# Two groups of transposes and copies placed behind the first layer's router products

## The chip, the cores and the metric

The kernel runs on one core of one Trainium2 chip. A core has five engines that this text names: TensorE (PE; its weight loads are listed apart as PEld), VectorE (DVE), ScalarE (ACT), GpSimd (POOL) and SyncE (SP), whose queue issues most DMAs. Each engine works through its own list of instructions in order and waits for others by semaphores. The metric is the device time of one launch in microseconds (us), less is better; a median of several runs is given.

## The reference, cut to what matters

The program computes two layers of a graph network on 3125 nodes with 256 features each. A layer adds a graph convolution and an attention part to the stream `x`, then a mixture of experts. What is computed around the change is the end of the first layer's graph and attention part and the start of its experts:

```python
xn = _layernorm(x, axis=-1)
x = x + _L0_gnn_ref(xn, ...) + _L0_mix_ref(xn[None], ...)[0]
x = x + _L0_ffn_ref(_layernorm(x, axis=-1)[None], ...)[0]

def _L0_ffn_ref(x, Wr, br, W1, b1, W2, b2, gamma, beta):
    logits = jnp.mean(x, axis=1) @ Wr + br             # mean over all 3125 rows
    routing_weights = jax.nn.softmax(logits, axis=-1)
    scale = jnp.where(expected_loads > capacity, capacity / expected_loads, 1.0)
    routing_weights = jax.nn.softmax(routing_weights * scale, axis=-1)
    top_w, top_i = jax.lax.top_k(rw_tok, 2)
    top_w = jax.nn.softmax(top_w, axis=-1)
    h = jax.nn.gelu(xf @ W1[e] + b1[e], approximate=False)   # for the chosen experts
    y = h @ W2[e] + b2[e]
    out = _layer_norm(weighted sum of y + x, gamma, beta)
```

The router sees the mean of all normalised rows, so all rows choose the same two of the eight experts, and nothing of an expert's product can start before the mean over all rows is known.

## The kernel before, in words

The 3125 rows are 25 tiles of 128 rows (`T` = 25), in five groups of five (`GROUP`, `GROUPS`). `X` holds the stream, `N` the normalised rows with nodes on the partitions, `NT` the same rows transposed, with features on the partitions (`KC` = 2 blocks of 128 features). `ps` are eight banks of PSUM: three (`TA`, handed out in turn by `A.next()`) take the transposes and the experts' first products, two (`TV`) take products that VectorE adds to the stream, one (`PACC`) takes sums that stay.

The stage around the change closes the graph convolution's second hop, group by group, on four engines at once:

- VectorE closes the hop of a group, adds TensorE's products for the group before it to `X` (L1723), takes the rows' statistics (L1445 to L1450), and writes the normalised rows of the group before that into `N` (L1456), each tile telling `xn_ready`.
- ScalarE applies the relu (L1280), takes the square root for the statistics (L1221), and copies transposed rows from PSUM into `NT` (`transposed_copies`, L1231), five tiles a group. Each copy frees its bank (`pa_free`) and then tells `nt_ready`.
- TensorE runs a loop over s = 0 to 6 (`for s in range(GROUPS + 2)`). For s below 5 it multiplies the hop's rows of group s by the layer's weights (`hops_out`, L947). For s of 2 and more it first transposes the normalised rows of group s - 2 (`normalised_transposed`, L818: two transposes for a tile, behind a wait for `xn_ready` and for a free bank), then adds the same rows to the column sums in `PACC` (L959: two products of 128x128 by 128x1 for a tile, listed as four matmuls, since an f32 product is two passes). In the last two turns, s = 5 and 6, there is no hop product left, only transposes and column sums of groups 3 and 4.

Then follows the router, a chain that no engine can shorten by overlap. TensorE tells `route_mm`; VectorE scales the column sums into `ybar` (L1757); TensorE multiplies them by the router's weights (L967); VectorE adds the bias, asks ScalarE for an exponential (`softmax`, L1733 to L1738, ScalarE's side is `exp`, L1226), limits the weights to the capacity, does a second softmax with a second exponential, finds the best two (L1772, L1773), asks for a third exponential (of one number for each partition, L1774) and computes the row numbers of the two experts' weights (L1780 to L1782). GpSimd then issues 16 gathers of weights (L770); the first three (two of the first layer's weights, one of biases) let TensorE start the first expert's first product (L981), the others the second expert and the second layer. TensorE waits for all `nt_ready` of the pass ahead of L981, since its moving operand is `NT`. The third exponential's answer is needed only for the scaling of the second layer's weights (L1787 to L1792), which stands behind the last of these gathers.

ScalarE's list in this stretch is: relu, root and copies for s = 0 to 6, then `exp`, `exp`, `exp`, then the gelu of L981's products (L1310).

Of the kernel before, what the change touches and what calls it, by code (L numbers as in the profile page):

```python
# [36 lines left out]
T = -(-NODES // P)  # L37
# [20 lines left out]
GROUPS = T // GROUP  # L58
# [53 lines left out]
def build(nc, a, out):  # L112
    with ExitStack() as ctx:
# [3 lines left out]
        def sem(name):  # L117
            return ctx.enter_context(nc.semaphore(name))
# [57 lines left out]
        xn_ready, nt_ready = sem("xn_ready"), sem("nt_ready")  # L176
# [196 lines left out]
        def group(g):  # L373
            return range(g * GROUP, (g + 1) * GROUP)
# [427 lines left out]
        def _(pe):  # L802
# [10 lines left out]
            def normalised_transposed(first, g, src=N):  # L813
                for t in group(g):
                    pe.wait_ge(xn_ready, first * T + t + 1)
                    o = A.next()
                    for c in range(KC):
                        mm = nc.tensor.transpose(o[:, c * P:(c + 1) * P], src[:, t, c * P:(c + 1) * P], ident[:, :])  # L818
                    mm.then_inc(pa_full, 1)
# [121 lines left out]
            def hops_out(t):  # L941

                if t % GROUP == 0:
                    pe.wait_ge(relu_ready, t // GROUP + 1)
                o = V.next()
                for c in range(KC):
                    mm = nc.tensor.matmul(o[:, 0:D], AT[:, c, t * P:(t + 1) * P], wgT[:, c, :], start=(c == 0), stop=(c == KC - 1))  # L947
                mm.then_inc(pv_full, 1)

            for s in range(GROUPS + 2):  # L950
                if s < GROUPS:
                    for t in group(s):
                        hops_out(t)
                if s >= 2:
                    normalised_transposed(1, s - 2)

                    for t in group(s - 2):
                        for c in range(KC):
                            mm = nc.tensor.matmul(PACC[:, c:c + 1], N[:, t, c * P:(c + 1) * P], valid[:, t:t + 1],  # L959
                                                  start=(t == 0 and c == 0), stop=(t == T - 1), skip_group_check=True)  # L960
# [5 lines left out]
            for c in range(KC):  # L966
                mm = nc.tensor.matmul(PACC[:, 8:8 + E0], ybar[:, c, :], wr[:, c, :], start=(c == 0), stop=(c == KC - 1))  # L967
            mm.then_inc(route_mm, 1)
            pe.wait_ge(nt_ready, 2 * T)
            first_done = [0] * GROUPS  # L970
            for g in range(GROUPS + 1):
# [240 lines left out]
        def _(act):  # L1212
# [4 lines left out]
            def root(v):  # L1217

                roots[0] += 1
                act.wait_ge(asked, roots[0])  # L1220
                nc.scalar.activation(v, v, ACT.Sqrt).then_inc(answered, 1)  # L1221

            def exp(v):
                roots[0] += 1
                act.wait_ge(asked, roots[0])
                nc.scalar.activation(v, v, ACT.Exp).then_inc(answered, 1)  # L1226

            def transposed_copies(tiles):
                for t in tiles:
                    o = A.next()  # L1230
                    nc.scalar.copy(NT[:, :, t * P:(t + 1) * P], o[:, 0:D].rearrange("p (c n) -> p c n", n=P)).then_inc(pa_free, 1)  # L1231
                    act.wait_ge(pa_free, A.n)
                    act.sem_inc(nt_ready, 1)
# [42 lines left out]
            for s in range(GROUPS + 2):  # L1276
                if s < GROUPS:
                    act.wait_ge(slice_ready, GROUPS + s + 1)
                    part = AT[:, 0:KC, s * GN:(s + 1) * GN]
                    nc.scalar.activation(part, part, ACT.Relu).then_inc(relu_ready, 1)  # L1280
                if 1 <= s <= GROUPS:
                    root(rstd[:, (s - 1) * GROUP:s * GROUP])
                if s >= 2:
                    transposed_copies(group(s - 2))


            exp(sc[:, 0:8])
            exp(sc[:, 0:8])
            exp(sc[:, 40:41])
            def squares(src, tiles, dump):  # L1290

                for t in tiles:
                    st.settle()
                    st.add(nc.scalar.activation(dump, src[:, t, :], ACT.Square, accum_out=rn[:, t:t + 1]))
# [853 lines left out]
```

## Time and profile before

| what | us |
|---|---|
| median of 3 runs (lowest, highest) | 2977.78 (2976.58, 2977.94) |
| the profiled execution's own time | 2973.64 |
| its span, from the first to the last instruction | 2971.8 |
| PE busy | 2477.6 (83% of the span) |
| DVE busy | 1303.0 (44%) |
| POOL busy | 884.5 (30%) |
| ACT busy | 454.1 (15%) |

The mean granted TensorE clock was 0.922 of full speed. In the rows below each line gives a start, a duration, the engine, the line of the kernel, the operation, what it writes and reads, the shape and how many instructions were merged (x20); in brackets stands how long the engine was idle before it and what released it. The clock column (PEclk) is 1.00 at TensorE's upper level of 2.4 GHz and 0.50 at its lower level of 1.2 GHz.

### The profile page before, as it was taken

Reading aid. Unit: us, or ns where it says so; the run is one execution under the profiler, and the core shown is the slowest. Engines: PE = TensorE matmul, PEld = TensorE weight load, DVE = VectorE, ACT = ScalarE, POOL = GpSimd, SP = SyncE. Lnnn points to the kernel's source line nnn. Section 1 sums busy time; section 2 is a strip of 40 time slices with the busy share of each in tenths; the row PEclk is TensorE's granted clock in tenths of the full one; section 3 lists DMA queues with packets and bytes.
Section 4 is the critical chain, followed back from the end, with each engine's and each line's share of the span. In section 5 each row is a group of like instructions: output and inputs, shape, how many; then the busy total and the mean of one; then the engine's idle time right before and its main releaser. Section 6 shows DMA issues by size and latency. Waiting matters only on the chain.

```text
span 2971.8 us, 33705 instructions
## 1 busy us (share of the span) xinstructions
PE 2477.6 (83%) x12264; PEld 1722.4 (58%) x12264; DVE 1303.0 (44%) x3539; ACT 454.1 (15%) x963; POOL 884.5 (30%) x917
## 2 busy tenths in 40 slices
PE   4567777776766766589969998999999998999999
PEld 3455655655555555567845565565555556566665
DVE  8887867766765757433482214131000003131221
ACT  0211110111000000022331103330000010413222
POOL 0177777774777777320030000120000000000000
PEclk9989998997888879769989999999999999989999
DMA  3134344343344344210022220022111000000001
GB/s 105 57 100 135 103 138 139 105 140 109 104 140 140 104 140 125 72 49 1 18 76 71 79 77 29 32 99 65 50 51 56 29 1 21 1 11 11 11 11 44
DMA packets 77650, 211.87 MB, mean 71 GB/s; under 512 B 16445, under 2 KB 33845, under 8 KB 76073
## 3 DMA queue, kind: packets, MB, share of 16 engines
q0 software_dynamic: 40800, 111.47, 12.7%
q1 hardware_dynamic: 36681, 98.17, 10.0%
q8 instruction: 103, 1.69, 0.2%
q14 instruction: 66, 0.54, 0.1%
HBM read 169.10 MB, written 40.47 MB: 71 GB/s over the span
## 4 chain that ended last, share of the span: by engine, by line
PE 64%; DVE 16%; DMA 7%; issue 5%; POOL 3%; ACT 2%; DVEq 1%; SPq 0%; ACTq 0%; POOLq 0%
PE ps L1114 16%; PE ps L1150 13%; DMA rows<-table,src_i 7%; PE ps L555 7%; PE ps L1086 7%; PE ps L1208 5%; POOL rows L494 3%; PE ps L981 3%; PE ps L992 3%; DVE onehot L674 2%; DVE NN L1671 2%; DVE NN L1659 2%; PE ps L880 1%; DVE NN L1660 1%; DVE NN L1682 1%
## 5 line engine op out<-in xcount | busy, mean ns | idle before, releaser
L494 POOL DMA_INDIRECT rows<-table,src_i x832 | 812.5, 977 | 389.2 <-issue 296.6
L555 PE MATMUL ps<-onehot,rows 128*128 128x128 f32 x3328 | 551.1, 308 | 212.4 <-DMA rows<-table,src_i 178.0
L555 PEld LDWEIGHTS ps<-onehot,rows 128*128 128x128 f32 x3328 | 524.3, 220 | 319.5 <-issue 206.2
L1114 PE MATMUL ps<-AS,WA 128*128 128x400 f32 (+1 forms) x768 | 259.7, 501 | 11.5 <-ACT NN L1352 5.1
L880 PE MATMUL ps<-NN 128*128 128x500 bf16 x416 | 170.7, 410 | 114.9 <-DVE NN L1660 99.4
L674 DVE TENSOR_SCALAR onehot<-iota_w,rel,wgt 128x128 f32<-128x128 f32 x848 | 231.1, 358 | 2.8 <-DVE iota_w L714 1.6
L1114 PEld LDWEIGHTS ps<-AS,WA 128*128 128x128 f32 x768 | 148.6, 194 | 121.4 <-issue 5.8
L1114 PE MATMUL ps<-NN,WA 128*128 128x400 f32 (+1 forms) x640 | 213.3, 495 | 1.0 <-ACT rows L1365 0.7
L2086 DVE SCALAR_TENSOR_TENSOR X<-ps,WA,X 128x256 f32<-128x256 f32 x150 | 72.5, 484 | 272.0 <-PE ps L1208 272.0
L1352 ACT ACTIVATE AS<-ps,small 128x400 f32<-128x400 f32 (+1 forms) x224 | 131.2, 586 | 334.4 <-PE ps L1114 334.4
L1114 PEld LDWEIGHTS ps<-NN,WA 128*128 128x128 f32 x640 | 122.1, 191 | 89.0 <-issue 1.3
L2030 DVE SCALAR_TENSOR_TENSOR AS<-ps,small,AS 128x408 f32 x32 | 20.3, 643 | 347.2 <-PE ps L1150 346.4
L692 DVE TENSOR_TENSOR AS<-AS,ps 128x256 f32 x104 | 43.8, 421 | 279.7 <-PE ps L555 279.7
L1671 DVE TENSOR_TENSOR NN<-NN,ps 128x500 f32 x208 | 140.0, 673 | 53.4 <-issue 22.6
L1659 DVE TENSOR_SCALAR NN<-WB,AS 128x500 bf16<-128x500 f16 x416 | 150.3, 361 | 0.3
L1150 PE MATMUL ps<-WA,NN 128*128 128x408 bf16 x768 | 137.1, 336 | 0.0
L1150 PE MATMUL ps<-onehot,NN 128*128 128x408 bf16 x768 | 136.1, 336 | 0.0
L1208 PE MATMUL ps<-WA,AS 128*128 128x256 f32 x600 | 135.5, 388 | 0.0
L880 PEld LDWEIGHTS ps<-NN 128*128 128x128 bf16 x416 | 43.9, 105 | 138.7 <-DVE NN L1671 97.8
L1208 PEld LDWEIGHTS ps<-WA,AS 128*128 128x128 f32 x600 | 104.0, 191 | 31.5 <-issue 13.2
L1660 DVE TENSOR_SCALAR NN<-WB,AS 128x128 bf16<-128x128 f16 x416 | 113.7, 273 | 0.0
L1723 DVE TENSOR_TENSOR X<-X,ps 128x256 f32<-128x256 f32 x100 | 41.2, 417 | 162.4 <-PE ps L1170 112.2
(353 smaller groups left out, 3055.2 us busy)
## 6 DMA issues: line engine op xcount, KB each, us to landing
adjacency<-NN SPq DMA_DIRECT2D x8, 2550.0 KB, 9.1
onehot<-adjacency SPq DMA_DIRECT2D x40, 510.0 KB, 3.5
WA<-adjacency SPq DMA_DIRECT2D x40, 510.0 KB, 3.5
rows<-table,src_i POOLq DMA_INDIRECT x832, 2.8
table<-NN SPq DMA_DIRECT2D x10, 640.0 KB, 3.3
table<-WA SPq DMA_DIRECT2D x25, 256.0 KB, 2.0
WA<-in_experts SPq DMA_DIRECT2D x6, 768.0 KB, 4.1
X<-in_x SPq DMA_DIRECT2D x1, 3072.0 KB
```

The lines of the kernel that those rows point to most:

```text
L494: nc.gpsimd.indirect_dma_start(slot_of(h, j, k), None, table[h - 1][:, :], bass.IndirectOffsetOnAxis(index, 0)).then_inc(gathered[h - 1][( ...
L555: mm = nc.tensor.matmul(EDGE[j % 2][:, c * P:(c + 1) * P], row[:, c * P:(c + 1) * P], onehot[:, j % 2 * U + k, :], start=(k == 0 and c == ...
L674: nc.vector.tensor_scalar(onehot[:, buffer * U + k, :], iota_w[:, :], rel[:, bass.ds(c, 1)], wgt[:, bass.ds(c, 1)], ALU.is_equal, ALU.mult ...
L880: nc.tensor.matmul(build_bank(s)[:, 0:CELLS], sources_in[:, n % CELL_RING, :], cells[:, n % CELL_RING, :], start=(j == 0), stop=(j == 1)). ...
L1086: mm = nc.tensor.matmul(EDGE[c][:, 0:SLABW], rows16, pieces[i % 4][:, n, :], start=(t == 0 and part == 0), stop=(t == T - 1 and part == 2))
L1114: mm = nc.tensor.matmul(o[:, 0:n.stop - n.start], weights[:, k, c * P:(c + 1) * P], src[:, k, n], start=(k == 0), stop=(k == chunks - 1))
L1150: mm = nc.tensor.matmul(banks[c][:, 0:SLABW], hidden16(t)[:, part, f], pieces[i % 4][:, n, :], start=(t == 0 and part == 0), stop=(t == T ...
L1208: mm = nc.tensor.matmul(o[:, 0:D], h2[:, k, t * P:(t + 1) * P], w[:, 2, k, :], start=(k == 0), stop=(k == KC - 1))
L1352: nc.scalar.activation(dst[:, c, n], o[:, 0:n.stop - n.start], ACT.Relu, bias=bias[:, c:c + 1]).then_inc(pa_free, 1)
L1659: nc.vector.tensor_scalar(cells[:, n % CELL_RING, :], iota500, cell_of[:, n:n + 1], None, ALU.is_equal).then_inc(cells_ready, 1)
L1660: nc.vector.tensor_scalar(sources_in[:, n % CELL_RING, :], iota500[:, 0:P], source_in[:, n:n + 1], None, ALU.is_equal).then_inc(cells_read ...
L1671: nc.vector.tensor_tensor(part, part, build_bank(s)[:, 0:CELLS].rearrange("p (t n) -> p t n", n=SUBW), ALU.add).then_inc(slab_added, 1)
```

## The change

In TensorE's loop the transposes of groups 3 and 4 are left out (`2 <= s < GROUPS` covers groups 0 to 2 only) and stand behind the router's products instead. The column sums stay, and since no transposes with their wait stand ahead of them now, each tile's column sums get a wait of their own for `xn_ready` (in all five groups). ScalarE's ten copies of groups 3 and 4 move too: two tiles behind the first exponential, the other eight behind the second one, ahead of the third.

```diff
@@ TensorE @@
                     for t in group(s):
                         hops_out(t)
+                if 2 <= s < GROUPS:
+                    normalised_transposed(1, s - 2)
                 if s >= 2:
-                    normalised_transposed(1, s - 2)
-
                     for t in group(s - 2):
+                        pe.wait_ge(xn_ready, T + t + 1)
                         for c in range(KC):
                             mm = nc.tensor.matmul(PACC[:, c:c + 1], N[:, t, c * P:(c + 1) * P], valid[:, t:t + 1],
                                                   start=(t == 0 and c == 0), stop=(t == T - 1), skip_group_check=True)
...
             mm.then_inc(route_mm, 1)
+            for g in range(GROUPS - 2, GROUPS):
+                normalised_transposed(1, g)
             pe.wait_ge(nt_ready, 2 * T)
@@ ScalarE @@
                 if 1 <= s <= GROUPS:
                     root(rstd[:, (s - 1) * GROUP:s * GROUP])
-                if s >= 2:
+                if 2 <= s < GROUPS:
                     transposed_copies(group(s - 2))


             exp(sc[:, 0:8])
+            transposed_copies(group(GROUPS - 2)[0:2])
             exp(sc[:, 0:8])
+            transposed_copies(group(GROUPS - 2)[2:])
+            transposed_copies(group(GROUPS - 1))
             exp(sc[:, 40:41])
```

## Rows read from the trace of the kernel before

**Rows 1.** The page's chain of waits by engine, over the whole span.
```profile
PE 64%; DVE 16%; DMA 7%; issue 5%; POOL 3%; ACT 2%; DVEq 1%; SPq 0%; ACTq 0%; POOLq 0%
```

**Rows 2.** The chain of waits in order of time, 1292.71 to 1358.63 (start, us, what).
```profile
1292.71 2.13 PE ps L959 x20
...
1296.81 4.06 PE ps L959 x20
1300.87 2.24 PE ps L818 x10
1303.10 4.07 PE ps L959 x20
...
1308.82 12.43 issue
1321.25 37.38 PE ps L981 x128
```

**Rows 3.** Timeline of GpSimd: the first and the third gather of the experts' weights.
```profile
1316.15 0.94 POOL L770 DMA_INDIRECT WA<-in_w_rows,small  x1 [88.59 <-DVEq L1784]
...
1318.65 0.94 POOL L770 DMA_INDIRECT small<-in_b_rows,small  x1 [0.30 <-issue]
```

**Rows 4.** Timeline of VectorE, 1295 to 1340.
```profile
1295.91 1.71 DVE L1456 TENSOR_SCALAR NN<-X,small 128x256 f32<-128x256 f32 x5
...
1315.37 0.15 DVE L1787 TENSOR_SCALAR small<-small 128x1 f32<-128x1 f32 x1
...
1339.04 0.75 DVE L1792 TENSOR_SCALAR WA<-WA,small 128x1024 f32<-128x1024 f32 x1 [23.12 <-DMA rows<-in_b_rows,small]
```

**Rows 5.** Timeline of ScalarE, 1301 to 1332.
```profile
1301.43 2.31 ACT L1231 COPY NN<-ps 128x256 f32<-128x256 f32 x5 [3.97 <-PE ps L818]
1303.84 1.28 ACT L1226 ACT_TABLE_LOAD   x1
1309.46 0.21 ACT L1226 ACTIVATE small<-small 128x8 f32<-128x8 f32 x1 [4.33 <-DVE small L1734]
1311.53 0.21 ACT L1226 ACTIVATE small<-small 128x8 f32<-128x8 f32 x1 [1.87 <-DVE small L1734]
1313.04 0.20 ACT L1226 ACTIVATE small<-small 128x1 f32<-128x1 f32 x1 [1.30 <-DVE small L1774]
...
1331.75 0.53 ACT L1310 ACTIVATE AS<-ps,small 128x320 f32<-128x320 f32 x1 [0.55 <-PE ps L981]
```

**Rows 6.** Busy time and granted clock by stretches; the first line names the columns.
```profile
core 0: us, PE busy (x) PEld busy (x) DVE busy (x) ACT busy (x) POOL busy (x), PEclk, DMA share, GB/s
...
1257.00:1261.50 4.50, 0.26 (x2) 0.00 (x0) 4.39 (x16) 0.21 (x1) 0.00 (x0) 1.00 0.00 0
1262.00:1263.40 1.40, 0.00 (x0) 0.00 (x0) 1.40 (x2) 0.00 (x0) 0.00 (x0) 0.50 0.00 0
1238.10:1241.20 3.10, 3.10 (x8) 2.47 (x9) 1.91 (x2) 1.27 (x1) 0.00 (x0) 0.50 0.00 0
...
1295.50:1296.00 0.50, 0.46 (x4) 0.20 (x2) 0.46 (x3) 0.39 (x2) 0.00 (x0) 0.96 0.88 353
...
1296.50:1301.00 4.50, 4.50 (x24) 4.50 (x23) 1.12 (x4) 0.75 (x2) 0.00 (x0) 0.50 0.20 79
...
1321.20:1326.20 5.00, 4.95 (x10) 3.22 (x11) 0.00 (x0) 2.11 (x3) 3.78 (x5) 0.50 0.47 132
```

**Rows 7.** Timeline of TensorE's weight loads, 1300 to 1303.
```profile
1300.52 2.18 PEld L818 LDWEIGHTS ps<-ident,NN 128*128 128x128 f32 x10
```

**Rows 8.** Timeline of ScalarE, 1597 to 1605: a copy that stands between two exponentials.
```profile
1604.25 0.27 ACT L1337 COPY VB<-ps 128x128 f32<-128x128 f32 x1
1604.67 0.31 ACT L1226 ACTIVATE WA<-WA 128x128 f32<-128x128 f32 x1 [0.16 <-DVE WA L1883]
```

**Rows 9.** Busy time of the engines over the rest of the span (columns as in Rows 6).
```profile
1358.47:2971.80 1613.33, 1550.95 (x7042) 974.10 (x7040) 387.02 (x903) 324.10 (x686) 55.08 (x55) 0.97 0.12 39
```

## The prediction

> **What bounds the kernel now.** I read the chain of waits by engine first: TensorE holds 64% of it, VectorE 16% [rows 1]. Shares of the whole span don't price this change, because it touches one stretch of about 30 us; so I next read the chain in order of time there [rows 2]. The reader is to see one unbroken string: column sums of group 2 to 1294.84, then transposes of group 3 (to 1296.81, so 1.97 us), column sums of group 3 (4.06), transposes of group 4 (2.24), column sums of group 4 (4.07, ending at 1307.17), then VectorE's `ybar`, the router's four matmuls (ending at 1308.82), and 12.43 us in which TensorE stands still until L981. The view gives that gap to "issue", since DMA completions of this kind aren't linked to it. Its content is in the other engines' timelines. VectorE and ScalarE do two softmaxes and the indices; GpSimd's first gather waits for VectorE (L1784) until 1316.15, the third is issued by 1319.59 [rows 3], and 1.66 us behind that L981 starts. So L981 is released by the gathers, and the gathers by the column sums. What makes the column sums end earlier makes everything behind them start earlier.
>
> VectorE is no limit to the column sums: its last normalised row of group 4 is written by 1297.62 [rows 4], while TensorE works on those sums until 1307.17. In this stretch the transposes of groups 3 and 4 thus lie on the path that sets the end, though nobody needs them before L981.
>
> **The change, part by part.**
>
> *Transposes out of the path.* 1.97 us (group 3) and 2.24 us (group 4) leave the string [rows 2]: 4.21 us. That would be all, if the clock stood still. The same 20 matmuls of L959 took 2.13 us for group 2 and 4.06 us for group 3 [rows 2]; in between the granted clock fell from the upper level (2.4 GHz) to the lower (1.2 GHz), where it is from 1296.5 on [rows 6]. The half microsecond to 1296.0 still has 0.96, so the fall is at 1296.0. From 1294.84 to 1296.0 TensorE did transposes, which were held up by banks and by VectorE and gained little from the clock. After the change it does column sums there: 1.16 us at 2.13/20 = 0.107 us each is 11 of the 40 matmuls. The 29 left take 0.203 us each, 5.9 us, and the sums end at 1296.0 + 5.9 = 1301.9 instead of 1307.17. Gain: 5.2 us. Rows must be there: group 3's are written before 1295.91, group 4's by 1297.62 [rows 4], and TensorE reaches group 4's first tile about 1297.8; no wait binds.
> Bounds by the place of the fall. If the clock is already low at 1294.84, the two transposed groups are worth 2 x 2.24 = 4.5 us. If it falls near 1298, both kernels do most of group 3's sums at the upper level and the gain is 6.0. If it stayed high in both, the new sums would be held by VectorE and end near 1297.62 + 4 x 0.107 + some tenths, hence about 1299.1 with TensorE's own 4.3 us of work, against 1303.0 for the string of before: 3.9.
>
> *Waits added.* 25 waits for `xn_ready`, one a tile; what queues behind each is that tile's weight loads and sums. In groups 0 to 2 the transposes ahead of them have already waited for the same count. The trace has no row of L959 behind a wait, but one of L818, whose every tile has two: its weight loads for group 4 began at 1300.52, while the sums ahead of them ran until 1300.87 [rows 2, 7], so a wait that is already met doesn't stop the loading ahead. I take 0. Upper bound, if each wait lays one load bare at the lower level: 2.18/10 = 0.22 us [rows 7], for ten tiles on the path 2.2 us. A gain from a wait is excluded, it only delays.
>
> *Transposes and copies put back in the gap.* Behind the router's products TensorE runs 20 transposes: at the lower level 0.45 us a tile (2.24/5), 4.5 us of the 12.43 us gap. Three tiles go through at once, then banks pace them by ScalarE's copies, 2.31/5 = 0.46 us each [rows 5]. With R for the end of the router's products (before: 1308.82): the first exponential was at R + 0.64 to R + 0.85, and by then tile one is transposed (R + 0.45). Two copies end at R + 1.8. The second exponential was asked and began at R + 2.71: ScalarE is free 0.9 us ahead of it, so the path has nothing to pay. It ends at R + 2.92; eight copies end at R + 6.7. L981 is released at R + 12.4, so the copies are 5.7 us ahead of its wait for `nt_ready`. What pays is the third exponential: from R + 4.2 to about R + 6.8. VectorE reached the line that needs it at 1315.37 = R + 6.55 [rows 4], so it waits some 0.3 us; behind that it had 23.12 us of idle time until the second layer's weights land [rows 4], and the row numbers for the gathers stand ahead of this wait. Cost on the path 0. Were the cover gone, that delay would be the price: 0.3 us. Below nothing isn't possible, as no one waits less for it. No DMA is issued or moved by the edit, and SP's and GpSimd's lists are untouched.
>
> *Table load.* ScalarE loads its table ahead of the first exponential, at 1303.84, behind group 4's copies [rows 5]. Now it follows the last root, near 1294.3, and is even less on the path: 0.
> A reader might fear that copies between exponentials make ScalarE load a table twice more, 1.28 us each [rows 5]. At 1604.25 a copy stands right ahead of an exponential, with 0.16 us between them and no load [rows 8]; I take 0, with 2.6 us (two loads) as the other end.
>
> *What happens behind.* L981 starts 5.2 us earlier, at 1316.0. It starts at the lower level, which lasted over 5.0 us [rows 6], and its 32 banks took 37.38 us [rows 2] where banks at the upper level come every 0.53 + 0.55 = 1.08 us [rows 5], 34.5 in all: the cold start costs 2.9 us. Elsewhere a busy TensorE was granted the upper level again just after 3.1 us at the lower [rows 6], so the same start can cost about 1.6. The shift can thus bring up to 1.3 us more; I take 0, since before was near the long end in one execution and the timed runs average over it. Behind L981 TensorE is busy for 1551 of 1613 us [rows 9], and every gap there hangs on work that starts with L981; I see no transfer or engine that keeps its old time, and take the shift as whole.
>
> Sum: 4.21 (transposes) + 1.0 (sums done at the upper level in their place) + 0 + 0 + 0 = 5.2 us. The profiled execution's own time is 2973.64 us, so 2968.4 for one like it. The median of the runs is 2977.78, 4.1 us above it, so the timed forecast is 2977.8 - 5.2 = 2972.6 us. Faster or slower by over 0.2% means 5.96 us (2971.8, 2983.7), about what a measurement of this kernel can tell from no change; my number lies just inside it.
>
> **The rivals.**
>
> *The filled gap keeps the clock up.* TensorE's transposes now fill about 5.7 us of the gap. If the clock rose in them and held until L981, its cold start would vanish: 2.9 us more, 8.1 in all, 2969.7 us. Against it: at 1257 to 1261.5 the clock stayed high over some 4 us of idle TensorE and was low by 1262 [rows 6], and 6.7 us of idle are left between the last transpose and L981.
> The Trainium skill, "TensorE: Matmul & The Clock Gate", section "HAM oscillation — how this bites in real kernels", says that idle gaps send the array back to its lower clock and the next burst starts cold; by that rule a shorter gap is the only way to keep it, and the trace agrees as far as the fall at 1262 goes.
>
> *The shift is lost on the way.* Behind L981 lie 1613 us with gaps of TensorE at many places (62 us in all [rows 9]), after which the clock falls and rises at places that move with the shift. Each such start differs by up to 1.3 us, as worked out above. Three or four of them the wrong way take 4 us: 2976 to 2978 us. For it: the profiled execution and the median differ by 4.1 us with the same program. Against it: the three runs agree within 1.4.
>
> *ScalarE is late for the second exponential.* If the two copies wait for TensorE's transposes (say each tile takes 0.9 instead of 0.45 us, with semaphores), they end at R + 2.8 rather than R + 1.8; the path pays 0.1 to 1 us, with a doubled table load up to 2.6. Gain 2.6 to 4.6: 2973 to 2975 us. Against it: 0.9 us of slack, and copies had such a pace at 1301.43.
>
> *Slower: the waits break TensorE's weight loading.* Place: L959. If a wait, even a met one, stops the loading ahead and the matmul ahead must drain too, a tile pays a load and a matmul: 0.22 + 0.20 us, 25 tiles 10.5 us, against 5.2 gained: 2983 us. It decides from 0.21 us a tile on, if all 25 lie on the path; in groups 0 to 2 VectorE's sums to `X` hide part. Against it: the row of L818's loads above.
>
> **How the numbers follow.** Forecast 0.64, own range 2971.0 to 2974.5 (gain 3.9 to 6.0 by the place of the fall, up to 1.3 by L981's start, 0.5 for the runs); 0.22 of it lies below 2971.8. Clock kept up: 0.10. Lost on the way: 0.14. ScalarE late: 0.07. Slower than before: 0.05, of which half goes past 0.2%; the other half stays within. Faster by over 0.2%: 0.22 + 0.10 = 0.32. Slower: 0.03. Within: 0.65. The range reaches from 2969.0, to hold the clock rival, to 2977.0, to hold most of the lost shift and ScalarE late.
>
> **What would show it.** In the profile after: no L818 between 1294 and the router's products; L959 in one string of 60 matmuls ending near 1302, its last 29 or so at 0.2 us; `ybar` at 1302, the router's matmuls ending near 1303.6; two copies between the first two exponentials, with no table load beside them; the last copy by 1310.4; L981 at 1316, still cold; VectorE's L1787 a few tenths late. It is wrong if L959 takes over 0.25 us a matmul at the lower level (the waits), if the gap ahead of L981 is longer than 12.4 us (ScalarE or the copies), or if L981 starts near 1316 and the end doesn't come 5 us earlier (lost on the way).

## The result, and the profile after

The changed kernel takes 2971.74 us (median of 16 runs, 2968.98 to 2974.85), the kernel before on the same chip 2976.53 (16 runs, 2972.51 to 2978.27). The medians are 4.8 us apart. The ratio on record is not that of the two medians: it is 0.9986, 95% interval 0.9979 to 0.9992, hence 4.2 us less, between 2.4 and 6.3. The forecast was 2972.6 and a shift of 5.2. The profiled execution took 2970.61 us, its span is 2968.7, against 2973.64 and 2971.8.

Code lines below the edit have new numbers: the column sums are L960 (before: L959), the router's products L968 (L967), L981 and L992 are now L984 and L995, and the copies' and exponentials' lines L1234 and L1229 (L1231, L1226).

The chain of waits of the changed kernel in order of time, the answer to [rows 2]:
```profile
1293.09 9.48 PE ps L960 x60
1302.60 0.50 DVE rows L1763 x2
1303.20 1.04 PE ps L968 x4
...
1314.08 2.67 DMA small<-in_b_rows,small
1316.74 0.09 issue
1316.83 36.40 PE ps L984 x128
```
The string of five pieces has become one of 60 matmuls. This time the view also names what the gap ahead of the expert's products was: it runs through the gathers, and the landing of the biases' rows ends it.

TensorE's timeline of the changed kernel:
```profile
1291.26 1.83 PE L818 MATMUL ps<-ident,NN 128*128 128x128 f32 x10
1292.93 9.63 PE L960 MATMUL ps<-small,NN 128*128 128x1 f32 x60
1303.20 1.02 PE L968 MATMUL ps<-small,rows 128*128 128x8 f32 x4 [0.64 <-DVEq L1765]
1304.08 2.54 PE L818 MATMUL ps<-ident,NN 128*128 128x128 f32 x10
1307.56 2.60 PE L818 MATMUL ps<-ident,NN 128*128 128x128 f32 x10 [0.94 <-ACT NN L1234]
1316.83 36.40 PE L984 MATMUL ps<-NN,WA 128*128 128x320 f32 x128 [6.68 <-DMA small<-in_b_rows,small]
```
From the start of group 2's transposes to the router's first product it is 1303.20 - 1291.26 = 11.94 us; before it was 16.92 (1290.88 to 1307.80). I call this stretch the string from here on. The moved transposes take two bursts with a wait for ScalarE between them, and 6.7 us of idle time stay behind them.

ScalarE's timeline, the answer to [rows 5]:
```profile
1294.62 1.28 ACT L1229 ACT_TABLE_LOAD   x1
1304.86 0.21 ACT L1229 ACTIVATE small<-small 128x8 f32<-128x8 f32 x1 [8.95 <-DVE small L1740]
1304.97 0.84 ACT L1234 COPY NN<-ps 128x256 f32<-128x256 f32 x2
1306.94 0.21 ACT L1229 ACTIVATE small<-small 128x8 f32<-128x8 f32 x1 [1.13 <-DVE small L1740]
1307.06 3.75 ACT L1234 COPY NN<-ps 128x256 f32<-128x256 f32 x8
1310.92 0.20 ACT L1229 ACTIVATE small<-small 128x1 f32<-128x1 f32 x1
```
ScalarE was idle for 1.13 us between the second copy and the second exponential, which follows the first by 2.08 us as before (2.07 [rows 5]); there is no further table load. The eight copies end 6.0 us ahead of L984. VectorE waits for the third exponential, the cost that was to be hidden, and is (timeline of VectorE):
```profile
1311.16 0.15 DVE L1793 TENSOR_SCALAR small<-small 128x1 f32<-128x1 f32 x1 [0.51 <-ACT small L1229]
1334.32 0.75 DVE L1798 TENSOR_SCALAR WA<-WA,small 128x1024 f32<-128x1024 f32 x1 [22.56 <-DMA rows<-in_b_rows,small]
```
The clock, from the view of stretches (columns as in [rows 6]): it is at 1.00 in the sums' first 3 us, at 0.50 by 1296.8, and still at 0.50 when L984 starts.
```profile
1293.10:1296.10 3.00, 3.00 (x29) 3.00 (x29) 2.89 (x15) 2.44 (x5) 0.00 (x0) 1.00 0.68 204
1296.80:1302.50 5.70, 5.70 (x28) 5.67 (x27) 1.20 (x4) 0.00 (x0) 0.00 (x0) 0.50 0.17 64
...
1316.80:1320.20 3.40, 3.37 (x7) 2.23 (x8) 0.00 (x0) 0.81 (x1) 2.60 (x3) 0.50 0.53 155
```

The two profiled executions, piece by piece: the stretch began 0.38 us later (its start lies anywhere from 1290.48 to 1293.74 us in the traces of the experiments below, so this is no effect of the change that could be told from chance), the string is 4.98 us shorter, from the router's first product to the expert's first 0.18 longer (13.63 against 13.45), the expert's first 32 banks 0.98 shorter (36.24 against 37.22, less time at the lower clock), and all that follows 2.30 longer (1615.6 us from the first second-layer product to the end, against 1613.3). Sum: -3.1 us, the difference of the spans.

### The profile page after: what moved, and what is told of

Read it like the earlier page. It is cut to its first block, busy times and chain, and to the rows that moved or that the text cites. A ratio compares the mean times of both kernels' runs of the same rounds, so it can differ in the third digit from the quotient of the medians.

```text
span 2968.7 us, 33705 instructions
## 1 busy us (share of the span) xinstructions
PE 2483.6 (84%) x12264; PEld 1722.8 (58%) x12264; DVE 1302.5 (44%) x3539; ACT 453.9 (15%) x963; POOL 884.5 (30%) x917
## 4 chain that ended last, share of the span: by engine, by line
PE 64%; DVE 17%; DMA 7%; issue 5%; POOL 3%; ACT 2%; DVEq 1%; SPq 0%; ACTq 0%; POOLq 0%
PE ps L1117 16%; PE ps L1153 13%; DMA rows<-table,src_i 7%; PE ps L555 7%; PE ps L1089 7%; PE ps L1211 5%; POOL rows L494 3%; PE ps L984 3%; PE ps L995 3%; DVE NN L1677 2%; DVE onehot L674 2%; DVE NN L1665 2%; PE ps L880 1%; DVE NN L1666 1%; DVE NN L1688 1%
## 5 line engine op out<-in xcount | busy, mean ns | idle before, releaser
L1117 PE MATMUL ps<-AS,WA 128*128 128x400 f32 (+1 forms) x768 | 259.9, 501 | 11.4 <-ACT NN L1358 4.9
```

What stands on the lines that cost most here:

```text
L1117: mm = nc.tensor.matmul(o[:, 0:n.stop - n.start], weights[:, k, c * P:(c + 1) * P], src[:, k, n], start=(k == 0), stop=(k == chunks - 1))
```

## The experiments

Each kernel ran in five rounds beside the kernel before on one chip, in four sessions; the median of the kernel before went from 2974.90 to 2978.95 between them, so a median is compared only with one that ran beside it. e0 is the changed kernel again; e1 and e9 are edits of the kernel before, all others of the changed one. The stretches of the table are read from TensorE's timeline of each profile; "string" and "to expert" as above, "banks" is from the first product of the expert's first layer to the first of its second, "rest" from there to the end of the span. The interval is that of the ratio to before.

| kernel | string | to expert | banks | rest | median us / before | interval |
|---|---|---|---|---|---|---|
| before | 16.92 | 13.45 | 37.22 | 1613.3 | | |
| changed | 11.94 | 13.63 | 36.24 | 1615.6 | 2971.74 / 2976.53 | 0.9979 to 0.9992 |
| e0_after (changed again) | 12.20 | 13.58 | 36.00 | 1615.4 | 2972.00 / 2976.94 | 0.9977 to 0.9995 |
| e1_waits_only | 16.92 | 13.55 | 37.06 | 1613.1 | 2974.40 / 2974.90 | 0.9990 to 1.0008 |
| e2_group4_only | 14.90 | 13.55 | 36.51 | 1612.6 | 2971.70 / 2974.90 | 0.9978 to 0.9996 |
| e3_copies_first | 12.01 | 16.42 | 36.48 | 1612.5 | 2972.56 / 2974.90 | 0.9982 to 1.0000 |
| e4_copies_last | 11.94 | 13.41 | 36.35 | 1612.3 | 2969.86 / 2974.90 | 0.9972 to 0.9990 |
| e5_group2_too | 11.63 | 13.41 | 36.53 | 1612.6 | 2971.55 / 2976.94 | 0.9970 to 0.9988 |
| e7_gap_filled | 12.76 | 13.63 | 34.60 | 1615.5 | 2971.07 / 2976.94 | 0.9968 to 0.9988 |
| e9_before_wide | 12.50 | 13.25 | 35.95 | 1615.4 | 2972.18 / 2978.95 | 0.9968 to 0.9986 |
| e6_wide_sums | 9.17 | 13.19 | 37.50 | 1613.5 | 2966.73 / 2976.94 | 0.9947 to 0.9974 |
| e10_wide_again | 9.17 | 13.21 | 37.38 | 1613.4 | 2968.85 / 2978.95 | 0.9958 to 0.9979 |
| e8_wide_filled | 9.17 | 13.19 | 34.60 | 1613.4 | 2965.86 / 2978.95 | 0.9946 to 0.9973 |

(For e5 the string is counted from the start of group 2's column sums, which follow the last hop product there; in the others group 2's transposes do.)

**Do the added waits cost?** The kernel before with the waits alone:
```diff
                     for t in group(s - 2):
+                        pe.wait_ge(xn_ready, T + t + 1)
                         for c in range(KC):
```


> The kernel before with only the 25 added waits of TensorE ahead of the column sums. Theory (the gain is the 4.2 us of transposes that left the string, plus sums at the higher clock): nothing but noise, the column sums of a group stay at 2.1 us at the upper level and 4.1 us at the lower one, and the time stays within 1 us of before. Rival (the waits stop TensorE's loading ahead, and the change would have gained more without them): 0.1 to 0.4 us more a tile, so a group's sums take 2.6 us or more at the upper level and 5 or more at the lower one, and the time is 2 to 7 us above before.


The string is 16.92 us, to the hundredth that of before, and TensorE's timeline has the sums at their old lengths:
```profile
1293.86 2.29 PE L960 MATMUL ps<-small,NN 128*128 128x1 f32 x20
...
1297.92 4.27 PE L960 MATMUL ps<-small,NN 128*128 128x1 f32 x20
```
The median is 0.5 us below before. The rival that was to make the change slower is out.

**Is the gain the transposes'?** One group moved instead of two (TensorE's part of the edit to the changed kernel; ScalarE's copies follow it):
```diff
-                if 2 <= s < GROUPS:
+                if 2 <= s <= GROUPS:
                     normalised_transposed(1, s - 2)
...
-            for g in range(GROUPS - 2, GROUPS):
+            for g in range(GROUPS - 1, GROUPS):
                 normalised_transposed(1, g)
```


> Only group 4's transposes and copies follow the router's products; group 3's stay in the loop (two of group 4's copies between the first two exponentials, three behind the second). Theory: only 2.2 us leave the string, because the clock falls at about the same place and group 4's transposes were done at the lower level; the router's products end some 14.1 to 14.6 us after the start of group 2's transposes on TensorE's list (before 17.9, after 13.0, both with the start of line 818 for group 2 as zero, so between 15.5 and 15.9 if the string's other parts keep their time), and the time is about 2.2 us below before. Rival (the gain is the clock's placing, not the transposes): anything from 0 to 5 us, without relation to the 2.2.


The first figure of that expectation (14.1 to 14.6) is a slip of mine; 17.9 less 2.2 is the 15.7 of its second half. Measured to the end of the router's products it is 15.9 us, and the string is 2.02 shorter than before. The median is 3.2 below before, where 2.2 was said. Group 3's move is then worth 14.90 - 11.94 = 2.96. Its transposes take 1.91 us here (from their start to that of the sums behind them), so about 1 us is left for sums done at the upper clock in their place.

**How much room has ScalarE?** Its ten copies placed in two other ways:
```diff
             exp(sc[:, 0:8])
-            transposed_copies(group(GROUPS - 2)[0:2])
+            transposed_copies(group(GROUPS - 2))
+            transposed_copies(group(GROUPS - 1))
             exp(sc[:, 0:8])
-            transposed_copies(group(GROUPS - 2)[2:])
-            transposed_copies(group(GROUPS - 1))
             exp(sc[:, 40:41])
```


> The changed kernel, but all ten copies of groups 3 and 4 stand between the first and the second exponential. Theory (0.9 us of slack is all that ScalarE has ahead of the second exponential): two copies ended 1.1 us ahead of it, ten take 4.6 us and are paced by TensorE's transposes, so the second exponential comes about 2.6 to 3 us later than in the changed kernel, and the gathers and L981 with it: from the end of the router's products to L981 15.2 to 15.6 us instead of 12.6. Time about 2.8 us above the changed kernel, 2 us below before. Rival (ScalarE's place in the chain doesn't matter, the gathers' landing or nt_ready sets the end): 12.6 us as in the changed kernel and the same time.


ScalarE's timeline of this kernel has the second exponential 4.95 us behind the first, where 2.08 were needed:
```profile
1304.15 0.21 ACT L1229 ACTIVATE small<-small 128x8 f32<-128x8 f32 x1 [9.02 <-DVE small L1739]
1304.27 4.71 ACT L1234 COPY NN<-ps 128x256 f32<-128x256 f32 x10
1309.10 0.21 ACT L1229 ACTIVATE small<-small 128x8 f32<-128x8 f32 x1
```
The stretch to the expert's first product is 2.8 us longer than in the changed kernel (16.42 against 13.63; from the end of the router's products 15.4, in the range that stood before the run). So the split of the copies round the exponentials is no ornament: done the simple way it gives back more than half of the string's gain. The median is 2.3 us below before, where 2 was said.

With all ten behind the third exponential (e4):


> The changed kernel, but all ten copies stand behind the third exponential. Theory: the copies end about 9.2 to 9.5 us after the router's products, 3 us ahead of L981, so the path has nothing to pay: 12.4 to 12.6 us from the router's products to L981, VectorE's wait of 0.51 us for the third exponential gone, and the same time as the changed kernel within 1 us. The gap of TensorE between its last transpose and L981 is 3 us or more shorter, so if a shorter idle stretch keeps the clock up, L981 starts at the upper level here and its 32 banks take 34.5 instead of 36.4 to 37.4 us. Rival (the copies are needed early, nt_ready becomes the bound): L981 starts later by the amount that the copies end late, 1 us or more.


The stretch is 13.41 us (12.4 from the end of the router's products), and the gap ahead of the expert is 4.0 us instead of 6.7. The clock is low at its start all the same and the banks take 36.35 us, as the transposes ahead of this gap had run at the lower level already. VectorE's wait for the third exponential is gone and buys nothing. It is as good a place as the changed kernel's.

**Is more of the same worth more?** Group 2's transposes moved as well (two of its tiles between the exponentials; the first of the edit's places):
```diff
-                if 2 <= s < GROUPS:
+                if 2 <= s < GROUPS - 1:
                     normalised_transposed(1, s - 2)
```


> The changed kernel, and group 2's transposes and copies follow the router's products as well (two tiles of group 2 between the first two exponentials, 13 tiles behind the second). Theory (TensorE's string is what counts, until VectorE's rows bind): group 2's transposes take 1.83 us, but group 3's rows come 1.3 us after group 2's sums could end, so only 0.5 to 1.3 us are gained: the router's first product comes 10.7 to 11.4 us after the end of the last hop product's start where the changed kernel has 11.9. Fifteen tiles of copies end 9.3 us behind the router's products, 3 us ahead of L981. Time 0.5 to 1.3 us below the changed kernel. Rival (each group moved is worth its own 2 us): 2 us or more below the changed kernel. Rival (copies become late): 1 us or more above it.


The new bound shows in TensorE's timeline: it now waits for VectorE's rows of group 3.
```profile
1295.52 2.29 PE L960 MATMUL ps<-small,NN 128*128 128x1 f32 x20
1299.19 7.33 PE L960 MATMUL ps<-small,NN 128*128 128x1 f32 x40 [1.38 <-DVE NN L1463]
```
The string is 11.63 us, longer than the 10.7 to 11.4 that was said, and 0.3 to 0.6 us shorter than with two groups, at the lower edge of the expected 0.5 to 1.3; the medians of the two, on one chip, are 0.45 us apart and don't tell them apart.

**Why does the clock fall while TensorE is busy?** In all nine traces with one-column sums it fell inside them or in the transposes right behind. Here their moving operand is 128 columns wide, 127 of them for nothing (the line of the sums; with it VectorE reads the 128 equal columns, and the router's products go to another part of the bank):
```diff
-    mm = nc.tensor.matmul(PACC[:, c:c + 1], N[...], valid[:, t:t + 1], ...)
+    mm = nc.tensor.matmul(PACC[:, c * P:(c + 1) * P], N[...], valid[:, t:t + 1].to_broadcast([P, P]), ...)
```


> The changed kernel, but the column sums have a moving operand of 128 equal columns instead of one (the valid column repeated), so the sums come out already spread over 128 columns; the router's products go to another part of the bank. It tests why the clock falls in the sums: in five of six traces it fell about 2 to 4 us after the sums of group 2 or 3 had begun, with TensorE listed as busy. Theory (one column a pass counts for little, so the clock falls; the pace at the lower level, 0.203 us a pass, is the weight load): with 128 columns the clock stays at the upper level, a pass takes 0.11 to 0.13 us, the string of 60 passes takes 6.5 to 7.7 us instead of 9.5, and the router's first product comes 1.8 to 3 us sooner; time 2 to 3 us below the changed kernel. Rival (the columns don't matter to the clock, only add to the work): the clock falls as before, a pass takes 0.26 us at the lower level (as the 128x128 products of the edge pass do), the string takes 11.5 us or more, and the time is 2 us above the changed kernel.


TensorE's sums in its timeline (e10, the same kernel once more), and the stretches' view of e6:
```profile
1295.41 6.86 PE L960 MATMUL ps<-small,NN 128*128 128x128 f32 x60
```
```profile
1294.00:1300.80 6.80, 6.80 (x62) 6.71 (x60) 4.96 (x21) 2.61 (x5) 0.00 (x0) 1.00 0.54 188
1314.70:1320.10 5.40, 5.37 (x10) 3.53 (x11) 0.00 (x0) 2.34 (x3) 4.18 (x5) 0.50 0.52 133
```
The granted clock is 1.00 from end to end of the sums. In the chain of waits, which gave 2.13 us for 20 passes of one column at the upper level and 4.06 at the lower [rows 2], the 60 wide passes take 6.71 us: 0.112 us a pass, against 0.107 and 0.203. So the added columns are nearly free; the weight loads are listed as busy for 6.71 of the 6.80 us. The string is 9.17 us in both executions, 2.8 below the changed kernel's. In time e6 is 5.3 us below e0_after beside it, where 2 to 3 were said: the string is 3.0 shorter than that one's and the rest 1.9, the banks are 1.5 longer, and a part stays unexplained.


> The changed kernel with column sums of 128 columns once more, beside the other two on one chip, since it had only five timed runs. Theory: the clock is up through the whole string again, the router's first product 9.2 to 9.4 us behind the start of group 2's transposes, and the time 6 to 10 us below before. Rival (the clock's stay was luck in the first trace): it falls in the sums again, and the first product comes 11 us or more behind that start.

The same in the order of before (e9) separates the clock from the move:


> The kernel before, with its order as it was, and only the column sums made 128 columns wide. Theory: the clock stays at the upper level, so the string is group 2 to 4's transposes at 1.7 to 2.0 us each and sums at 2.3 us each, 12.4 to 13.2 us from the start of group 2's transposes to the router's first product instead of 16.9: 4 us below before from the clock alone. Against the kernel with the move and wide sums (9.3 us) that leaves 3 to 4 us for the move when the clock is up, less than the 5.0 it gave when the clock fell. Time 4 to 5 us below before. Rival (the move is what keeps the clock up, the columns alone don't): the clock falls as in before, and the time is within 1 us of it.


TensorE's timeline of it has every group at its upper-level length:
```profile
1297.48 2.40 PE L959 MATMUL ps<-small,NN 128*128 128x128 f32 x20
1299.72 1.83 PE L818 MATMUL ps<-ident,NN 128*128 128x128 f32 x10
1301.38 2.40 PE L959 MATMUL ps<-small,NN 128*128 128x128 f32 x20
```
The string is 12.50 us: 4.4 less than before, from the wide sums alone. With the move it is 9.17, so the move is worth 3.3 us when the clock is up and 5.0 when it falls. Each works without the other, but they overlap: both together take 7.75 us off the string, and not 5.0 + 4.4. In time e9 is 6.8 us below before (4 to 5 were said) and e10 10.1 (6 to 10).

**Does a filled gap keep the clock up for the expert?** Eight matmuls (16 passes) that nobody reads, behind the moved transposes:
```diff
                 normalised_transposed(1, g)
+            for n in range(8):
+                nc.tensor.matmul(EDGE[n % 2][:, 0:D], X[:, n, 0:P], X[:, n, :], start=True, stop=True)
             pe.wait_ge(nt_ready, 2 * T)
```


> The changed kernel with eight more matmuls (128x128 by 128x256, two passes each, into a free bank, their results never read) behind the moved transposes, so that TensorE has work for about 5 to 7 us of the 6.7 us gap ahead of L981. The added work is not part of the computation. It tests the rival of the filled gap: the clock at L981's start is set by what TensorE did just ahead. Theory: the clock rises in the added matmuls and is at the upper level when L981 starts; its 32 banks take 34.5 to 35 us instead of 36.2, and the time is 1 to 2 us below the changed kernel. Rival (the clock falls or stays low whatever fills the gap): banks 36 to 37.4 us, no gain, and up to 0.6 us lost if the added matmuls end late.


TensorE's timeline of e7 shows where the added matmuls lie:
```profile
1312.18 4.51 PE L973 MATMUL ps<-X 128*128 128x256 f32 x16
```
The stretches' view of e7: the clock rises in the added matmuls, holds over 2.3 idle us, and the banks run at the upper level throughout.
```profile
1310.00:1314.00 4.00, 4.00 (x15) 2.86 (x15) 3.09 (x22) 2.56 (x8) 0.20 (x1) 0.50 0.01 2
1316.70:1319.00 2.30, 0.00 (x0) 0.00 (x0) 0.00 (x0) 0.00 (x0) 1.69 (x3) 1.00 0.42 115
1319.10:1353.60 34.50, 34.50 (x128) 24.27 (x129) 10.38 (x11) 17.42 (x32) 11.10 (x12) 1.00 0.20 54
```
The banks take 34.60 us, 1.4 less than e0_after's beside it. The median is 0.9 lower, inside the spread, and e7's own string was 0.56 us longer in its trace than e0_after's (12.76 against 12.20), which the added matmuls stand behind and can't have caused; the gain is read from the trace, not shown by the time. Both together (e8):


> The changed kernel with both: column sums over 128 columns, and eight added matmuls (results never read) in the gap ahead of L981. Theory: the two act on different stretches, so both gains come together: the router's first product 9.3 us behind the start of group 2's transposes (changed kernel: 11.9), L981's banks 34.6 to 35 us instead of 37.7 as in the kernel with wide sums alone. Time 1 to 3 us below the kernel with wide sums alone and 11 to 13 us below before. Rival (the added matmuls are too short at the upper level, which they now may start in, and leave an idle stretch in which the clock falls again): banks 36 us or more and no gain.


TensorE's timeline:
```profile
1295.00 6.86 PE L960 MATMUL ps<-small,NN 128*128 128x128 f32 x60
...
1308.84 5.06 PE L973 MATMUL ps<-X 128*128 128x256 f32 x16
1315.69 34.77 PE L986 MATMUL ps<-NN,WA 128*128 128x320 f32 x128 [1.79 <-issue]
```
Both gains stand side by side: 9.17 and 34.60 us. Its median is 2965.86 (5 runs), 3.0 below e10's on the same chip, and the ratio to before is 0.9960 (0.9946 to 0.9973). It is clear of before and of the changed kernel; its ratio is that of e6 (0.9961), so that it beats e6 and e10 is read from the banks (2.8 to 2.9 us) and not shown by the time.

## Why the prediction was right, and where it was off

*The transposes on the string.* Forecast 4.21 us for both groups and 1.0 for sums at the upper clock, 5.2 in all; measured 4.98 (4.72 in the second execution, whose string of 12.20 us missed the 11.9 that was expected of it). e2 gives the parts: 2.02 and 2.96. The clock fell between 1296.1 and 1296.8, about where it was put, and the last sum ended near 1302.6, 0.7 later than forecast, of which 0.4 is the stretch's own later start. One bound was too high: for a clock that stays up in both, the prediction had a gain of 3.9 us, with 1.97 us for a group's transposes; e9 and e10 give 3.3, as a group's transposes take 1.66 us there.

*The waits.* Taken at 0, they are 0 on the string (e1).

*ScalarE.* Two copies before the second exponential cost nothing, with 1.13 us to spare where 0.9 was said; e3 shows what is lost without that. VectorE's wait for the third exponential is 0.51 us, 0.3 was said; it is hidden behind 22.56 us of waiting for weights. No table was loaded anew. The Trainium skill, "ScalarE: Activation LUTs", section "Table sets: the hidden batching unit", says that copy is in every table set; the trace agrees, with ten copies among three exponentials and one load.

*The gap ahead of L981* was put at 12.43 us and is 12.6; most of the difference is in the landing of the gathers (5.26 us from the first one's issue to L984, against 5.10).

*The cold start* was taken as unchanged; it was 1.0 us shorter here (36.24 against 37.22), within the 1.3 that stood as its bound. The rival that the filled gap keeps the clock up didn't come true in the changed kernel: the moved transposes end 6.7 us ahead of the expert. Its mechanism is real, though, as e7 shows with 2.4 us of gap.

*The shift taken as whole* is the step that failed in size. In the profiled execution 2.30 us are given back behind the expert's first layer. One place of it can be seen: behind an idle stretch of 4.25 us in the second layer, the same 48 matmuls took 12.31 us before and 13.65 after. TensorE's timeline of before, and under it that of the changed kernel:
```profile
1490.20 12.31 PE L992 MATMUL ps<-WA,AS 128*128 128x256 f32 x48 [4.25 <-DVE NN L1723]
```
```profile
1484.80 13.65 PE L995 MATMUL ps<-WA,AS 128*128 128x256 f32 x48 [4.25 <-DVE NN L1729]
```
The stretches' view of both over the same 6 us, before and then after: the granted clock is 0.72 in the one and 0.50 in the other, with the idle time the same.
```profile
1489.50:1495.50 6.00, 5.30 (x17) 4.38 (x18) 5.30 (x14) 0.00 (x0) 0.00 (x0) 0.72 0.34 112
```
```profile
1484.10:1490.10 6.00, 5.30 (x13) 4.23 (x14) 5.30 (x14) 0.00 (x0) 0.00 (x0) 0.50 0.34 112
```
That is 1.3 us of the 2.3, and the mechanism of the rival "lost on the way", at one place instead of three or four; where the other 1.0 us is lost was not found. Over 13 profiled executions the rest is either 1612.3 to 1613.5 us (nine) or 1615.4 to 1615.6 (four), and this one place sorts them: the 48 matmuls take 12.02 to 12.31 us in the nine and 13.50 to 13.65 in the four. The second value was had by the changed kernel both times, but also by e9, whose order is that of before (the fourth is e7), and e4, with the changed order on TensorE, had the first. So it doesn't belong to the change; I read it as luck in where the clock's falls and rises land, and what picks the value was not tried. When the 48 matmuls start doesn't settle it: the four start 1484.80 to 1485.75 us into the span, but e10, one of the nine, starts at 1485.25.

*The time.* The differences of the medians, 4.8 and 4.9 us (e0_after), are near the 5 us of the string, but the intervals (2.4 to 6.3 in the first) would also hold the 3.1 of the two profiled executions, so that they come so near the forecast of 5.2 is in part luck. The time itself is 0.9 us under the forecast of 2972.6, although the shift was smaller: the kernel before had a median of 2976.53 over 16 runs, 1.25 below the 2977.78 of three runs that the forecast started from.

## What to carry to other kernels

Ahead of a serial chain (a reduction, a router, a gather), look at what else stands on the list of the engine that feeds it, and move what nobody needs yet into the gap that the chain leaves; then place the other engine's half of that work between the chain's own short steps, with the slack counted, or it comes back on the path (2.8 us here). The price of a moved piece depends on TensorE's clock, so read the granted clock of the stretch first: keeping that up was worth nearly as much as the move (4.4 and 5.0 us of the string, 7.75 together). A shift of 5 us in a kernel with many restarts behind it arrives only within two or three microseconds, so judge such a change by its own stretch in the trace and by many runs.

## What the runs showed of the hardware

- TensorE's clock can fall while TensorE is busy. In the changed kernel, with TensorE listed as busy without a break, the granted clock went from 2.4 to 1.2 GHz inside a string of 128x128 by 128x1 products, and passes from 0.107 to 0.203 us. In all nine traces with such products it fell inside them or in the transposes right behind; with 128 columns it stayed at 2.4 GHz in all four traces and passes took 0.112 us. More work a matmul made the string shorter, 6.86 us against 9.63.
- Work without use in a gap of TensorE can pay: in both kernels that had them, eight matmuls brought the clock up, it stayed up over 1.8 and 2.4 idle us, and the next 128 matmuls took 34.6 us instead of 36.0 to 37.5. Without them the clock was low at that start in all the other traces.
